# Self-attention of the second block: head-pair scores and maxima as couples of 64-row matmuls on the two halves of the array

## The reference

```python
def _attn(xq, xc, Wq, Wk, Wv, Wo, bo):
    q = (xq @ Wq).reshape(B, N, HEADS, D_HEAD)      # HEADS 16, D_HEAD 64
    k = (xc @ Wk).reshape(B, S, HEADS, D_HEAD)
    v = (xc @ Wv).reshape(B, S, HEADS, D_HEAD)
    scores = jnp.einsum('bnhd,bshd->bhns', q, k) * D_HEAD ** (-0.5)
    attn = jax.nn.softmax(scores, axis=-1)
    out = jnp.einsum('bhns,bshd->bnhd', attn, v).reshape(B, N, HEADS * D_HEAD)
    return out @ Wo + bo

x = _L0_xattn_ref(x, ctx_768, ...)                  # first block
x = _attn(_ln(x, g1, b1), _ln(x, g1, b1), Wq1, Wk1, Wv1, Wo1, bo1) + x
x = _attn(_ln(x, g2, b2), context, Wq2, Wk2, Wv2, Wo2, bo2) + x
x = _geglu_ff(_ln(x, g3, b3), Wp, bp, Wf, bf) + x
```

## Time and profile before

| what | value |
|---|---|
| median of 3 runs | 2672.1 us |
| profiled execution, its own time | 2671.83 us |
| its span in the trace | 2669.8 us |
| PE busy over the span | 2347.1 us, 88% |
| DVE, POOL, ACT busy over the span | 1765.2, 1257.3, 1174.4 us |
| mean granted TensorE clock | 0.964 of full |

### The profile page before, as it was taken

The page is one execution under the profiler, slowest core; times in us unless marked ns, Lnnn a source line. Parts: engine busy times, 40 slices in busy tenths (PEclk is TensorE's granted clock), DMA queues, the critical chain, the costliest instruction groups (busy, mean ns, idle before and its releaser), DMA issues. The chain is left out here.

```text
span 2669.8 us, 33283 instructions
## 1 busy us (share of the span) xinstructions
PE 2347.1 (88%) x12268; PEld 1936.5 (73%) x12268; DVE 1765.2 (66%) x2597; ACT 1174.4 (44%) x1858; POOL 1257.3 (47%) x1126
## 2 busy tenths in 40 slices
PE   4777689968999999999999999995799999969999
PEld 2566578856777777777777777774588888858888
DVE  4767545557777777777777777775555565565554
ACT  1333322225656565665656566562334444311211
POOL 3767522224655656565565656554244445351111
PEclk9889899979999999999999999997799999989999
DMA  1111112110000000000000000002112111130000
GB/s 56 31 58 56 48 49 75 47 39 25 17 21 22 16 29 17 29 17 21 22 16 29 17 29 17 21 15 77 36 43 73 57 50 57 47 101 32 26 31 32
DMA packets 80227, 99.91 MB, mean 37 GB/s; under 512 B 39809, under 2 KB 46593, under 8 KB 80065
## 3 DMA queue, kind: packets, MB, share of 16 engines
q1 hardware_dynamic: 80064, 97.78, 11.4%
HBM read 75.19 MB, written 21.76 MB: 36 GB/s over the span
## 5 line engine op out<-in xcount | busy, mean ns | idle before, releaser
L151 PE MATMUL PS<-R 128*128 128x512 f32 (+2 forms) x3124 | 1099.2, 352 | 143.1 <-POOL R L170 47.0
L152 PE MATMUL PS<-R 128*128 128x512 f32 (+2 forms) x3124 | 1071.2, 343 | 0.0
L153 PE MATMUL PS<-R 128*128 128x512 f32 (+2 forms) x3124 | 1069.2, 342 | 0.0
L164 POOL TENSOR_SCALAR R<-F 128x1024 fp32r<-128x1024 f32 (+1 forms) x608 | 641.5, 1059 | 705.3 <-DVE F L955 208.0
L151 PEld LDWEIGHTS PS<-R 128*128 128x128 f32 (+1 forms) x3124 | 601.3, 192 | 266.1 <-issue 64.5
L167 DVE TENSOR_TENSOR R<-F,R 128x1024 fp32r<-128x1024 f32 (+3 forms) x522 | 635.0, 1221 | 166.3 <-POOL R L164 163.7
L153 PEld LDWEIGHTS PS<-R 128*128 128x128 f32 (+1 forms) x3124 | 601.0, 192 | 69.4
L152 PEld LDWEIGHTS PS<-R 128*128 128x128 f32 (+1 forms) x3124 | 601.5, 193 | 64.3
L161 ACT ACTIVATE R<-PS 64x512 fp32r<-64x512 f32 (+3 forms) x780 | 426.9, 556 | 290.5 <-PE PS L153 213.0
L1252 ACT ACTIVATE F<-PS 128x1024 f32<-128x1024 f32 x256 | 263.2, 1028 | 334.6 <-PE PS L1114 202.3
L1333 DVE TENSOR_REDUCE F<-PS 128x2 f32<-128x1024 f32 x256 | 303.6, 1217 | 5.2 <-PE PS L1147 4.6
(11 more groups left out here) (71 smaller groups left out, 1710.0 us busy)
## 6 DMA issues: line engine op xcount, KB each, us to landing
F<-sd SPq DMA_DIRECT2D x256, 128.0 KB
xs<-F SPq DMA_DIRECT2D x32, 512.0 KB, 2.7
F<-xs SPq DMA_DIRECT2D x32, 512.0 KB, 3.3
F<-in_x SPq DMA_DIRECT2D x8, 512.0 KB, 3.3
F<-sd SPq DMA_DIRECT2D x16, 256.0 KB
out<-F SPq DMA_DIRECT2D x8, 512.0 KB, 2.6
F<-in_w_q SPq DMA_DIRECT2D x8, 256.0 KB, 3.1
F<-in_w_o SPq DMA_DIRECT2D x16, 128.0 KB, 2.1
```

What stands on the lines that cost most here:

```text
L151: nc.tensor.matmul(o, L[0], Rr[0], start=start, stop=False, skip_group_check=share)
L152: nc.tensor.matmul(o, L[0], Rr[1], start=False, stop=False, skip_group_check=share)
L153: return nc.tensor.matmul(o, L[1], Rr[0], start=False, stop=stop, skip_group_check=share)
L164: return nc.gpsimd.tensor_scalar(o, i, 1.0, 1.0, ALU.mult, ALU.mult)
```

## The change

The stacks go. Q and K of a pair are kept as they leave the projection, heads one above the other on the partitions: a high and a low array for each (`q3_s`, `k3_s`). A head's scores are then three products of 64 rows (high by high, high by low, low by high), taken from partitions 0 to 63 for head 0 and 64 to 127 for head 1. The code issues them in couples: head 0 on the upper half of the array, head 1 on the lower half, each into its own bank. Part 0 has six such matmuls instead of two. Part 1 subtracts the maximum with a matmul of one row, ones by the negative maximum (`one3`, `nm3`), on partition 0 for head 0 and 64 for head 1. `largest` becomes one couple of 64-row matmuls on the high parts instead of two of 128 rows; its matmul count stays. In the compiled program a 64-row matmul is marked as a tile of 64 rows by 128 columns and the one-row matmul as a tile of 32 rows by 128; all others of this part stay at 128 by 128. Counted in order over the whole program, the marked tile size changes 216 times before and 1187 times after.

ACT makes a pair's high parts with two copies of 128x512 and copies the negated maxima as one of 128x512; DVE makes the low parts with two subtractions of 128x512; POOL copies nothing for it; `clear` is gone. The events that counted halves now count pairs.

```diff
--- before.py
+++ after.py
@@ -372,7 +372,8 @@
 
         with nc.sbuf_tensor("R3", [128, 24700], FR) as r, nc.sbuf_tensor("F3", [128, NALL - 24700], FP) as g:
             ra, fa = Area(r, 24700), Area(g, NALL - 24700)
-            ka, kb, qa, qb = [[[ra.take(NT) for _ in range(2)] for _ in range(2)] for _ in range(4)]
+            q3_s, k3_s = [[ra.pair(NT) for _ in range(2)] for _ in range(2)]
+            nm3, one3 = [ra.take(NT) for _ in range(2)], ra.take(128)
             v3_s = [ra.pair(4, 2, 192) for _ in range(2)]
             P3 = ra.pair(4, 2 * NT)
             o3_s = [ra.pair(NT) for _ in range(2)]
@@ -1023,12 +1024,11 @@
         N3 = 8 * NB
         loop3 = range(-1, N3 + 4)
         W3q, W3k, W3v, W3o = place("q1"), place("k1"), place("v1"), place("o1")
-        top, low = slice(0, 64), slice(64, 128)
-        v3_set = event("v_set", 1)
+        head = (slice(0, 64), slice(64, 128))
+        v3_set, one3_set = event("v_set", 1), event("sel_set", 1)
         m3_set = event("m_set", 1)
-        qk_mm, q3_hi, q3_lo = event("qk_mm", 2 * N3), event("q_hi", 2 * N3), event("q_lo", 2 * N3)
-        k3_hi, k3_dup, k3_lo = event("k_hi", 2 * N3), event("k_set", 2 * N3), event("k_lo", 2 * N3)
-        k3_clear, k3_zero = event("k_clear", 2), event("k_zero", 2)
+        qk_mm, q3_hi, q3_lo = event("qk_mm", 2 * N3), event("q_hi", N3), event("q_lo", N3)
+        k3_hi, k3_lo = event("k_hi", N3), event("k_lo", N3)
         v3_mm, v3_hi, v3_lo = event("v_mm", N3), event("v_hi", N3), event("v_lo", N3)
         b3_mm, b3_max = event("b_mm", 4 * N3), event("b_max", 4 * N3)
         nm3_mm, nm3_neg = event("nm_mm", N3), event("nm_neg", N3)
@@ -1097,21 +1097,21 @@
 
         def pe_attention1():
             def scores(t, j, part):
-                i = t % 2
+                q, k, nm = q3_s[t % 2], k3_s[t % 2], nm3[t % 2]
                 kk = slice(128 * j, 128 * j + 128)
                 if part == 0:
-                    pe.wait_ge(q3_hi, 2 * t + 1)
-                    pe.wait_ge(q3_lo, 2 * t + 1)
-                    pe.wait_ge(k3_dup, 2 * t + 1)
-                    pe.wait_ge(k3_lo, 2 * t + 1)
-                    pe.wait_ge(k3_clear, i)
+                    pe.wait_ge(q3_lo, t)
+                    pe.wait_ge(k3_lo, t)
                     pe.wait_ge(e3, 4 * t + j - 1)
-                    for h in range(2):
-                        nc.tensor.matmul(bank(h), ka[i][h][:, kk], qa[i][h], start=True, stop=False)
+                    for kx, qx in ((0, 0), (0, 1), (1, 0)):
+                        for h, rows in enumerate(head):
+                            nc.tensor.matmul(bank(h), k[kx][rows, kk], q[qx][rows, :], start=kx + qx == 0, stop=False)
                 else:
                     pe.wait_ge(nm3_neg, t)
+                    pe.wait_ge(one3_set, 0)
                     for h in range(2):
-                        m = nc.tensor.matmul(bank(h), kb[i][h][:, kk], qb[i][h], start=False, stop=True)
+                        row = slice(64 * h, 64 * h + 1)
+                        m = nc.tensor.matmul(bank(h), one3[row, :], nm[row, :], start=False, stop=True)
                     m.then_inc(c3_mm.sem, 1)
 
             def project(u, n):
@@ -1138,13 +1138,11 @@
                 m.then_inc(v3_mm.sem, 1)
 
             def largest(u, q, b0):
-                i = u % 2
-                pe.wait_ge(q3_hi, 2 * u + 1)
-                pe.wait_ge(q3_lo, 2 * u + 1)
-                pe.wait_ge(k3_hi, 2 * u + 1)
-                pe.wait_ge(k3_lo, 2 * u + 1)
-                for h in range(2):
-                    m = nc.tensor.matmul(bank(b0 + h), qa[i][h][:, 128 * q:128 * q + 128], ka[i][h], start=True, stop=True)
+                pe.wait_ge(q3_lo, u)
+                pe.wait_ge(k3_lo, u)
+                for h, rows in enumerate(head):
+                    m = nc.tensor.matmul(bank(b0 + h), q3_s[u % 2][0][rows, 128 * q:128 * q + 128],
+                                         k3_s[u % 2][0][rows, :], start=True, stop=True)
                 m.then_inc(b3_mm.sem, 1)
 
             def values(d, j):
@@ -1234,16 +1232,12 @@
 
         def act_attention1():
             def project(u, n):
-                i, src = u % 2, bank(2 + n)
                 act.wait_ge(qk_mm, 2 * u + n)
+                act.wait_ge(c3_mm, 4 * (u - 2) + 3)
                 if n == 0:
-                    act.wait_ge(c3_mm, 4 * (u - 2) + 3)
-                    for h in range(2):
-                        act_copy(qa[i][h][top, :], src[64 * h:64 * h + 64, :])
-                        act_copy(qa[i][h][low, :], src[64 * h:64 * h + 64, :]).then_inc(q3_hi.sem, 1)
+                    act_copy(q3_s[u % 2][0], bank(2)).then_inc(q3_hi.sem, 1)
                 else:
-                    for h in range(2):
-                        act_copy(ka[i][h][top, :], src[64 * h:64 * h + 64, :]).then_inc(k3_hi.sem, 1)
+                    act_copy(k3_s[u % 2][0], bank(3)).then_inc(k3_hi.sem, 1)
 
             def exponent(t, j):
                 n = 4 * t + j
@@ -1283,10 +1277,7 @@
                     if ok(u, N3) and j == 3:
                         act.wait_ge(nm3_mm, u)
                         act.wait_ge(c3_mm, 4 * (u - 2) + 3)
-                        act.wait_ge(k3_clear, u % 2)
-                        for h in range(2):
-                            m = act_copy(qb[u % 2][h][64:65, :], bank(6)[64 * h:64 * h + 1, :], scale=-1.0)
-                        m.then_inc(nm3_neg.sem, 1)
+                        act_copy(nm3[u % 2], bank(6), scale=-1.0).then_inc(nm3_neg.sem, 1)
                     if tail3(s, j) == 14:
                         for k, n in ((0, 128), (1, 64)):
                             act.wait_ge(ctx_tr, k)
@@ -1299,27 +1290,12 @@
 
         def dve_attention1():
             def project(u, n):
-                i, src = u % 2, bank(2 + n)
-                for h in range(2):
-                    hs = src[64 * h:64 * h + 64, :]
-                    if n == 0:
-                        dve.wait_ge(q3_hi, 2 * u + h)
-                        nc.vector.tensor_tensor(qb[i][h][top, :], hs, f32(qa[i][h])[top, :], ALU.subtract
-                                                ).then_inc(q3_lo.sem, 1)
-                    else:
-                        dve.wait_ge(k3_hi, 2 * u + h)
-                        nc.vector.tensor_tensor(ka[i][h][low, :], hs, f32(ka[i][h])[top, :], ALU.subtract
-                                                ).then_inc(k3_lo.sem, 1)
-
-            def clear(i):
-                for h in range(2):
-                    nc.vector.memset(f32(qb[i][h])[low, :], 0.0)
-                    m = nc.vector.memset(f32(kb[i][h])[low, :], 0.0)
-                m.then_inc(k3_zero.sem, 1)
-                dve.wait_ge(k3_zero, i)
-                for h in range(2):
-                    m = nc.vector.memset(f32(kb[i][h])[64:65, :], 1.0)
-                m.then_inc(k3_clear.sem, 1)
+                if n == 0:
+                    dve.wait_ge(q3_hi, u)
+                    dve_rest(q3_s[u % 2][1], bank(2), q3_s[u % 2][0]).then_inc(q3_lo.sem, 1)
+                else:
+                    dve.wait_ge(k3_hi, u)
+                    dve_rest(k3_s[u % 2][1], bank(3), k3_s[u % 2][0]).then_inc(k3_lo.sem, 1)
 
             def rests(n):
                 if 0 <= n < 4 * N3:
@@ -1349,8 +1325,6 @@
                         rests(4 * s - 1)
                     if ok(u, N3) and j == 0:
                         project(u, 1)
-                        if u < 2:
-                            clear(u)
                     if ok(u, N3) and j == 1:
                         s_ = v3_s[(u // 2) % 2]
                         src = bank(6).rearrange("p (t a e) -> p t a e", t=2, a=2)
@@ -1402,6 +1376,7 @@
 
         def pool_attention1():
             nc.gpsimd.memset(M3, 0.0).then_inc(m3_set.sem, 1)
+            nc.gpsimd.memset(f32(one3), 1.0).then_inc(one3_set.sem, 1)
             for i in range(2):
                 nc.gpsimd.memset(f32(v3_s[i][0][:, :, :, 64:128]), 1.0)
                 m = nc.gpsimd.memset(f32(v3_s[i][1][:, :, :, 64:128]), 0.0)
@@ -1411,10 +1386,6 @@
                 b, p = divmod(max(t, 0), 8)
                 more = t >= 0 and b + 1 < NB
                 for j in range(4):
-                    if ok(u, N3) and j == 0:
-                        for h in range(2):
-                            pool.wait_ge(k3_hi, 2 * u + h)
-                            pool_copy(kb[u % 2][h][top, :], f32(ka[u % 2][h])[top, :]).then_inc(k3_dup.sem, 1)
                     if ok(d - 1, N3) and j == 2:
                         f = d - 1
                         pool.wait_ge(in3[f % 2], 2 * (f // 2) + 1)
```

## The result

The changed kernel takes 2686.69 us, the median of 7 runs (2681.34 to 2691.09), against 2672.1 before in 7 runs. The ratio is 1.0054, with a 95% interval of 1.0039 to 1.0069: slower by 14.6 us. I had forecast slower by 70.

The account below looks back on a forecast made before the run. PE was taken to set the pace at full clock. Matmul savings against entry costs for changed tile sizes summed to +2.2 us per two steps, 32 x 2.2 = +70 on 2671.8, giving 2742 us; range 2655 to 2810.

Parts of the forecast that it names:

- C: Third of four stretches of PE's two-step period: from 7.11 to 8.3 us (+1.1).
- 0.31 us to enter a stretch of couples: On PE, cost of each entry to couples, their weight loads starting 0.11 us apart; 0.20 if side by side.
- A: First of four stretches of PE's two-step period: from 6.25 to 6.6 us (+0.4).
- B: Second of four stretches of PE's two-step period: from 11.85 to 12.0 us (+0.2).
- D: Fourth of four stretches of PE's two-step period: from 13.21 to 13.7 us (+0.5).
- floors: DVE's work keeps B from under 11.85 us; POOL's copies and DVE's sum keep D from much under 13.2.
- 2696: Forecast time with every entry at 0.20 us: A and C cost +0.75, B and D hide theirs, +24 us.
- rival (2): Faster, as changes of tile size cost little on PE: 2619 us if they cost nothing; chance 0.12.
- `clear` ran in two steps only; I count nothing for it: Dropping the `clear` calls, which ran in only two steps, was priced at nothing.
- ACT's relief: Fewer ACT copies: 2.9 us a step less, 1.8 ahead of the first exponential, ending waits on ACT in A and C.
- Rival (1): The couples' matmuls on PE don't overlap: 40 couples in two steps take 0.23 us more each, 2966 us; chance 0.18.
- (3): No change: at 0.12 us an entry, PE's work moves into the waits, -6 us, 2666; chance 0.08.

Follow-up runs that it names:

- e3: The changed kernel with part 0's six 64-row matmuls ordered head by head instead of in couples: 2686.04 us.
- e4: The kernel before, with the constant rows filled by POOL at the stage's start instead of by DVE in the first two steps: 2661.64 us.
- e1: The changed kernel with the one-row matmul made 64 rows deep, so scores and maxima share one tile size: 2667.4 us.
- e10: The changed kernel with the output's high part copied by ACT and the first quarter's scores merged ahead of Q's projection: 2662.93 us.
- e8: e1 with the attention output's high part copied by ACT and both parts of the first quarter's scores ahead of Q's projection: 2599.79 us.
- e6: e1 with the high part of the attention output copied by ACT instead of POOL: 2624.55 us.
- e5: The changed kernel with ACT's old load of 64-row copies for Q, K and the negated maxima put back: 2704.42 us.
- e12: e8 with ACT's old load put back as in e5: 2631.03 us.
- e2: The changed kernel with both matmuls of every couple on partitions 0 to 63: 3007.07 us.
- run 64: Not a run label but part of "run 64 rows deep": the changed kernel's one-row matmul made 64 rows deep, as in e1: 2667.4 us.

## Why the prediction was wrong, point by point

**Direction and mechanism held; the size of one term did not.** Couples overlap, changes of tile size cost time, PE stays the bound at a granted clock of 1.00, ACT's waits vanish and C loses most.

**The step that failed: "0.31 us to enter a stretch of couples".** I read the weight loads of the earlier trace rows, 0.11 us apart, and took it that the two loads of a couple come one after the other. Those loads followed one another on the same rows. On different halves they run side by side (two in 0.18 us), so the entry costs 0.09 + 0.11 = 0.20 as everywhere. With 0.20 the prediction's own sum gave A 6.3, C 7.8, and B and D held by their floors of 11.85 and 13.2: +24 us for the stage, "2696". Measured were 6.28, 7.77, 11.95 and 13.31, and +23.6 us. That the two totals agree so well is partly luck: B and D came out 0.2 us above the sum, and half of the other periods lose less than the one it was made for. I had this case worked out and chose against it with the argument that "the rows show loads one after another and none side by side", which was an argument from what the trace could not show.

The Trainium skill's statement that matmuls on distinct row groups start about 4 ns apart (TensorE: Matmul & The Clock Gate, Part 3) is what these traces show for float32r too, 3 to 4 ns in the couples and 10 ns in e3. I had used it for rival (2) only and not for the load.

**A term set to nothing: "`clear` ran in two steps only; I count nothing for it".** The opening got 6.6 us shorter, and e4 gives 5.5 of it to the fills on DVE. So +23.6 - 6.6 = +17, beside the measured +14.6; the rest is within what single executions differ by.

**The floors held.** B could not go under 11.85 and D not under 13.2: with eight changes less in them, e1 left both at 11.95 and 13.31, and what it gained in these two steps lies all in A and C. e10 against e8 shows that twelve changes cost 57 to 63 us once POOL's and DVE's chains are shorter, and e6 that B and D fall by 1.0 and 0.7 us. POOL's and DVE's idle time was no reserve; what they did in B and D was on the path.

**ACT's relief** was worth 18 to 21 us in this place (e5). That what the couples save on ACT, DVE and POOL is what makes the merged order pay is shown for ACT in part only (e12). Rival (1) has its price from e2: 3007 us, where I had 2966; some 45 us of it are a granted clock that fell, which I had priced at nothing. Rivals (2) and (3) did not happen, as the entry costs 0.20 and not 0.12.

**The range.** 2655 to 2810 held the time, but +70 was nearly five times the measured +14.6. Of the 55 us between them 46 are the one term of 0.11 us that comes 20 times in two steps (2742 against 2696), and 6.6 the opening.

## What to carry to other kernels

Here splitting the array into halves gave the overlap in full, in both orders of the two heads that were run; what it cost was 0.20 us at each change of tile size. So count the changes in the instruction stream first, and count them again when its order changes, make every small matmul of a stretch the same size (here by letting a one-row matmul run 64 rows deep over zeros) and put stretches together. Compare distances between starts too, since short waits do not show in the list of waits. Before pricing an edit on the busiest engine, find the stretches where another engine's chain sets the end: the same edit gave 16 us in one kernel and 57 to 63 in another, mostly by that (and by two changes more in two steps). The version to keep is e8, 2599.79 us, 2.6% under before.

## What the runs showed of the hardware

- Matmuls on rows 0 to 63 and rows 64 to 127 run side by side, and so do their weight loads; behind 128-row work six take 0.89 us in couples and 1.58 us on one half (the change and e2).
- Between the halves a matmul may start ahead of one that the program has earlier (e3: pairs 10 ns apart; inferred, since the records do not name the half).
- A change of tile size costs 0.20 us between matmuls of 256 or 512 columns, for 128 and 64, 64 and 32, and 32 and 128 rows alike, about 0.09 of it ahead of the first matmul of the new size and 0.11 behind it. Before matmuls of 64 columns only 0.11 showed.
- A 64-row ACT copy takes as long as one of 128 rows (0.592 and 0.598 us of mean in the earlier trace rows and the changed kernel), and a DVE subtraction too (0.688 and 0.691). Half-high instructions are paid in full.
- The same DVE subtraction of 128x1024 takes 1.2 us when it starts alone and 2.05 to 2.10 in the median when it starts during a POOL copy or subtraction (249 cases in the kernel before), and a POOL copy of 128x1024 takes 1.05 us alone and 1.98 in the median when it starts during such a subtraction.
- With the couples in series (e2) the granted clock, 1.00 in the change's steady part, was 0.97 over e2's, in falls of 3.4 us to the lower level.
